# A two-layer graph network on one core: warm-up matmuls, a re-ordered start, GpSimd in the x split, and the last block in column halves

## The reference

```python
deg = jnp.sum(adj, axis=1, keepdims=True) + 1e-05            # layer 0
out = (adj / deg) @ h @ W_neigh.T + b_neigh + h @ W_self.T + b_self
x = layernorm(x + relu(out))
d = rowsum ** (-0.5)  (0 where rowsum is 0)                   # layer 1
x = layernorm(x + relu((d[:, None] * adj * d[None, :]) @ x @ W + b))
```

## Time and profile before

| what | us |
|---|---|
| median of 3 runs (lowest, highest) | 800.73 (800.4, 802.11) |
| span of the profiled execution, first to last instruction | 800.8 |
| busy: TensorE, VectorE, ScalarE, GpSimd | 782.1, 577.4, 386.9, 0.3 |
| the chain that ended last: TensorE's share | 94% |

### The profile page before, as it was taken

The page is one execution under the profiler, slowest core; times in us unless marked ns, Lnnn a source line. Parts: engine busy times, 40 slices in busy tenths (PEclk is TensorE's granted clock), DMA queues, the critical chain, the costliest instruction groups (busy, mean ns, idle before and its releaser), DMA issues.

```text
span 800.8 us, 11034 instructions
## 1 busy us (share of the span) xinstructions
PE 782.1 (98%) x3704; PEld 653.0 (82%) x3704; DVE 577.4 (72%) x868; ACT 386.9 (48%) x528; POOL 0.3 (0%) x6
## 2 busy tenths in 40 slices
PE   7899999999999999999999999999999999999995
PEld 4678888888888888888888888888888888888884
DVE  5799989899898998989966554555546455554643
ACT  3463745536446364454554545445444544545451
POOL 0000000000000000000000000000000000000000
PEclk9999999999999999999999999999999999999998
DMA  8767574755647556465565575746575574657540
GB/s 258 274 252 239 179 244 154 253 183 166 236 155 236 193 174 236 157 233 189 181 227 165 175 255 174 250 162 237 180 236 187 171 246 162 236 180 239 180 158 27
DMA packets 54459, 160.93 MB, mean 201 GB/s; under 512 B 5024, under 2 KB 18464, under 8 KB 54432
## 3 DMA queue, kind: packets, MB, share of 16 engines
q1 hardware_dynamic: 46224, 152.46, 56.6%
q10 hardware_dynamic: 8208, 8.13, 2.9%
HBM read 152.17 MB, written 8.39 MB: 201 GB/s over the span
## 4 chain that ended last, share of the span: by engine, by line
PE 94%; DMA 2%; DVE 2%; ACT 1%; issue 0%; SPq 0%
PE ps_main L675 84%; PE ps_epi L613 8%; DMA raw<-adj_t 2%; PE ps_main L657 1%; PE ps_epi L634 1%; DMA tt<-x_nat 1%; DVE lo L389 0%; DVE acc L565 0%; ACT hi L256 0%; PE ps_epi L693 0%; DVE tt L436 0%; DVE stats L585 0%; DVE tt L419 0%; DVE xs L389 0%; ACT tt L359 0%
## 5 line engine op out<-in xcount | busy, mean ns | idle before, releaser
L256 ACT ACTIVATE hi<-raw 128x1024 fp32r<-128x1024 f32 x254 | 269.4, 1061 | 352.8 <-PE ps_main L675 327.8
L389 DVE TENSOR_TENSOR lo<-raw,hi 128x1024 fp32r<-128x1024 f32 x254 | 310.4, 1222 | 145.3 <-ACT hi L256 145.2
L675 PE MATMUL ps_main<-hi,xs 128*128 128x512 f32 x1136 | 366.3, 392 | 4.3 <-DVE lo L389 4.3
L675 PE MATMUL ps_main<-hi,zs 128*128 128x512 f32 x896 | 283.0, 390 | 0.0
L675 PEld LDWEIGHTS ps_main<-hi,xs 128*128 128x128 f32 x1136 | 214.2, 189 | 49.3 <-DVE lo L389 3.6
L675 PE MATMUL ps_main<-lo,xs 128*128 128x512 f32 x568 | 222.4, 392 | 0.0
L675 PEld LDWEIGHTS ps_main<-hi,zs 128*128 128x128 f32 x896 | 168.3, 188 | 34.3
L675 PE MATMUL ps_main<-lo,zs 128*128 128x512 f32 x448 | 174.7, 390 | 0.0
L565 DVE TENSOR_TENSOR acc<-acc,raw 128x1024 f32<-128x1024 f32 x112 | 136.3, 1217 | 0.0
L675 PEld LDWEIGHTS ps_main<-lo,xs 128*128 128x128 f32 x568 | 107.3, 189 | 20.0 <-issue 0.2
L675 PEld LDWEIGHTS ps_main<-lo,zs 128*128 128x128 f32 x448 | 84.2, 188 | 16.3
(11 more groups left out here) (74 smaller groups left out, 322.7 us busy)
## 6 DMA issues: line engine op xcount, KB each, us to landing
raw<-adj_t SPq DMA_DIRECT2D x256, 512.0 KB, 3.3
res<-x_nat SPq DMA_DIRECT2D x11, 512.0 KB, 6.4
xt_sb<-xt SPq DMA_DIRECT2D x8, 512.0 KB, 5.0
x_scratch<-tt ACTq DMA_DIRECT2D x8, 512.0 KB, 6.2
res<-x_scratch SPq DMA_DIRECT2D x8, 512.0 KB, 6.0
out<-tt ACTq DMA_DIRECT2D x7, 512.0 KB, 6.4
tt<-x_nat SPq DMA_DIRECT2D x4, 512.0 KB, 6.4
acc<-x_nat SPq DMA_DIRECT2D x2, 256.0 KB, 3.6
```

The source lines that it names most:

```text
L256: return act.activation(dst, src, ACT.Copy)
L389: return dve.tensor_tensor(dst, src, hi_part.bitcast(f32), ALU.subtract)
L675: last = pe.matmul(ps[:, f, :], stationary(layer, part, jt, f), mov[:, slot(u), cols], start=(jt == 0 and i == 0), stop=(jt == JT - 1 and ...
```

## The change

- TensorE first runs seven matmuls of zeros (512 columns) into `ps_main[1]`, which is overwritten later. VectorE clears the tile they read.
- The first transfer of `adj` becomes two halves of 256 KB, issued first on SyncE; the three pieces of x's chunk 0 (128, 128 and 256 KB) are issued by ScalarE. TensorE's first units wait piece by piece.
- Weights are loaded behind unit 8's transfer instead of unit 4's and split at unit 8, the biases behind unit 12's; `xt` at unit 11 instead of 8, used at 11 instead of 10.
- The `lo` parts of chunks 3, 5, 7 and 0 are subtracted by GpSimd. Chunk 0 is split at the end of the first block, since only the second block reads its split form; VectorE and TensorE wait for it there.
- The last four units of the last block are multiplied in two column halves (256 columns each). The first half's product with `W` and its rows are done while the second half is being multiplied; the second half of units 0 to 11 is kept in `xt` by ScalarE and added by VectorE.

```diff
+HB = IB // 2
+HT = TB // 2
+TAIL = NU - RING
+WARM = 7
...
+        on_dve, on_pool = (1, 2, 4, 6), (3, 5, 7, 0)
+
+        def wait_x_split(eng, c):
+
+            if c in on_dve:
+                eng.wait_ge(xl_ready, on_dve.index(c) + 1)
+            else:
+                eng.wait_ge(xl_ready_pool, on_pool.index(c) + 1)
...
-            return 10 if is_first(b) else 9
+            return 11 if is_first(b) else 9
...
-                        load_x_first(0)
+                        sp.dma_start(raw[:, 0, 0:IB], adj_in[0, 0, :, 0:IB]).then_inc(raw_head, 16)
+                        sp.dma_start(raw[:, 0, IB:UW], adj_in[0, 0, :, IB:UW]).then_inc(raw_full[0], 16)
+                        continue
...
-                        if u == 0:
-                            load_x_first(1)
-                        elif u % 2 == 1 and u < NU - 1:
+                        if u % 2 == 1 and u < NU - 1:
                             load_x((u + 1) // 2)
-                        if u == 4:
+                        if u == 8:
                             load_weights()
+                        if u == 12:
+                            load_biases()
...
+            for c in on_pool:
+                at = slice(c * XC, (c + 1) * XC)
+                pool.wait_ge(xh_ready, c if c else JT // XC)
+                pool.tensor_tensor(xs[:, at, 1, :], x_stage(c), xs[:, at, 0, :].bitcast(f32), ALU.subtract)\
+                    .then_inc(xl_ready_pool, 1)
...
-                        if u % 2 == 0:
+                        if u % 2 == 0 and u > 0:
                             c = u // 2
-                            if c == 0:
-                                for full in x_first_full:
-                                    act.wait_ge(full, 16)
-                            else:
-                                act.wait_ge(x_full[c % 2], 16 * ((c + 1) // 2))
+                            act.wait_ge(x_full[c % 2], 16 * ((c + 1) // 2))
                             split_hi(xs[:, c * XC:(c + 1) * XC, 0, :], x_stage(c)).then_inc(xh_ready, 1)
-                        if u == 7:
+                        if u == NU - 1:
+                            for full in x_first_full:
+                                act.wait_ge(full, 16)
+                            split_hi(xs[:, 0:XC, 0, :], x_stage(0)).then_inc(xh_ready, 1)
+                        if u == 8:
...
+                def stationary_hi(f):
                     act.wait_ge(half_done, f + 1)
-                    split_hi(st_hi[:, f, :], ps_main[1][:, f, :]).then_inc(sth_ready, 1)
-                act.wait_ge(root_ready, 2 * NB)
-                act.activation(root[:, 0:TB], root_in[:, 0:TB], ACT.Sqrt).then_inc(root_taken, 1)
-                act.wait_ge(norm_ready, 2 * NB)
-                for t in range(TB // 2, TB):
+                    split_hi(st_hi[:, f, 0:HB], ps_main[1][:, f, 0:HB]).then_inc(sth_ready, 1)
+
+                def keep_partial(f):
+                    act.wait_ge(stl_ready, 2 * NB + f)
+                    act.activation(partial(f), ps_main[1][:, f, HB:IB], ACT.Copy).then_inc(part_ready, 1)
+
+                def stationary_hi_late(f):
...
+            for i, at in enumerate((slice(0, 1), slice(1, 2), slice(2, XC))):
+                act.dma_start(x_stage(0)[:, at, :], x_nat[0, :, at, :]).then_inc(x_first_full[i], 16)
...
+                stationary_lo(0)
+                stationary_lo(1)
+                rows(0)
+                add_partial(0)
+                stationary_lo_late(0)
+                scales(0)
+                add_partial(1)
+                stationary_lo_late(1)
+                rows(1)
+                scales(1)
+                dve.wait_ge(norm_ready, 2 * NB + 1)
+                dve.tensor_scalar(tt[:, HT, :], tt[:, HT, :], rstd[:, HT:HT + 1], nmr[:, HT:HT + 1],
+                                  ALU.mult, ALU.add).then_inc(y_ready, 1)
...
+            dve.memset(xs[:, JT - 1, :, :].bitcast(f32), 0.0).then_inc(warm_set, 1)
...
+                if epi is None:
+
+                    pe.wait_ge(warm_set, 1)
+                    for _ in range(WARM):
+                        pe.matmul(ps_main[1][:, 0, :], xs[:, JT - 1, 0, 0:P], xs[:, JT - 1, :, :].rearrange("p a f -> p (a f)"),
+                                  start=True, stop=True)
+                elif layer == 0:
+                    wait_x_split(pe, 0)
...
+                def half_unit(h, f, u):
+                    if (h, f) == (0, 0):
+                        pe.wait_ge(z_ready, UJ * (u + 1))
+                        pe.wait_ge(l_ready, g0 + (u + 1))
+                    for q in range(UJ):
+                        jt = u * UJ + q
+                        cols = slice(q * IB + h * HB, q * IB + (h + 1) * HB)
+                        for i, (part, mov) in enumerate(((0, hi), (0, lo), (1, hi))):
+                            last = pe.matmul(ps_main[1 - h][:, f, 0:HB], stationary(1, part, jt, f),
+                                             mov[:, slot(u), cols], start=(h == 1 and jt == TAIL * UJ and i == 0),
+                                             stop=(jt == JT - 1 and i == 2))
+                    if u == NU - 1:
+                        last.then_inc(half_done, 1)
+
+                def half_product(h, k):
+                    pe.wait_ge(stl_ready, n + 1 + h * FH + k)
+                    for t in range(h * HT, (h + 1) * HT):
+                        for q, (st, part) in enumerate(((st_hi, 0), (st_hi, 1), (st_lo, 0))):
                             last = pe.matmul(ps_epi[:, t, 0:F], st[:, k, t * P:(t + 1) * P],
                                              moving_weight(1, part, k),
                                              start=(k == 0 and q == 0), stop=(k == FH - 1 and q == 2))
                         if k == FH - 1:
                             last.then_inc(tile_done, 1)
+
+                for f in range(FH):
+                    for u in range(TAIL, NU):
+                        half_unit(0, f, u)
+                half_unit(1, 0, TAIL)
+                half_unit(1, 0, TAIL + 1)
+                half_product(0, 0)
+                half_product(0, 1)
+                half_unit(1, 0, TAIL + 2)
+                half_unit(1, 0, TAIL + 3)
+                for u in range(TAIL, NU):
+                    half_unit(1, 1, u)
+                half_product(1, 0)
+                half_product(1, 1)```

What stands where on the engines that wait or are waited for follows. First VectorE in the first block, before, from unit 6's `lo` to unit 8's (`xs` is a chunk of x, `wn_sb` and `ws_sb` are the weights, `acc` the row sums):

```order
L389 TENSOR_TENSOR lo<-raw,hi 128x1024
L565 TENSOR_TENSOR acc<-acc,raw 128x1024
L389 TENSOR_TENSOR wn_sb<-xt_sb,wn_sb 128x512
L389 TENSOR_TENSOR ws_sb<-xt_sb,ws_sb 128x512
L389 TENSOR_TENSOR lo<-raw,hi 128x1024
L565 TENSOR_TENSOR acc<-acc,raw 128x1024
L389 TENSOR_TENSOR xs<-res,xs 128x4x256
L389 TENSOR_TENSOR lo<-raw,hi 128x1024
```

More of the change, by code:

```diff
@@ L237, in last_epilogue @@
                 load_residual(*epi)
-                for t in range(TB // 2):
-                    sp.wait_ge(y_ready, t + 1)
+                for t in range(HT):
+                    sp.wait_ge(x1_ready, (2 * NB - 1) * TB + t + 1)
                     sp.dma_start(out[NB - 1, t], tt[:, t, :]).then_inc(tt_stored, 16)
+                sp.wait_ge(y_ready, 1)
+                sp.dma_start(out[NB - 1, HT], tt[:, HT, :]).then_inc(tt_stored, 16)
                 sp.wait_ge(tt_stored, (2 * NB + TB) * 16)
@@ new lines, in last_epilogue @@
+                stationary_hi(1)
+                keep_partial(0)
+                keep_partial(1)
+                square_root(0)
+                stationary_hi_late(0)
+                stationary_hi_late(1)
+                normalise(0, 0)
+                normalise(0, 1)
+                square_root(1)
+                normalise(1, TB - 1)
+                act.wait_ge(x1_ready, (2 * NB - 1) * TB + HT + 1)
+                act.dma_start(out[NB - 1, TB - 1], tt[:, TB - 1, :]).then_inc(tt_stored, 16)
@@ new lines, in stationary_lo_late, with statistics, rows @@
+                def stationary_lo_late(f):
+                    dve.wait_ge(sth_ready, n + 1 + FH + f)
+                    split_lo(st_lo[:, f, HB:IB], whole(f), st_hi[:, f, HB:IB]).then_inc(stl_ready, 1)
+                def statistics(t):
+                    linked(but=1 if t % HT == 0 else 0)
+                    link(dve.bn_stats(stats[:, t, :], tt[:, t, :]))
+                def rows(h):
+                    t = h * HT
+                    scale_product(layer, n, t)
+                    scale_product(layer, n, t + 1)
+                    add_residual(n, t)
+                    add_residual(n, t + 1)
+                    statistics(t)
+                    statistics(t + 1)
+                    linked()
+                    dve.bn_aggr(mv[:, t, :], stats[:, t, :])
+                    link(dve.bn_aggr(mv[:, t + 1, :], stats[:, t + 1, :]))
+                    linked()
+                    at = slice(t, t + HT)
```

(25 more changed lines are left out.)

96 lines of the change are left out of this document (51 added, 45 removed).

## The result

The change made the kernel slower: 807.78 us as the median of 10 runs, against 800.8 for the kernel before, also of 10. I had forecast 794.1. The runs fall in two groups: two of the ten took 800.6 and 800.7 us, the other eight 807.1 to 810.4. Each run's time is about 1.8 us above its own span (808.36 against 806.5 for the profiled one).

What follows compares the result with a forecast made beforehand. TensorE was taken as the bound, so only the start and the end could give anything. The terms -2.1 - 6.5 + 2.7 - 0.8 = -6.7 us, against 800.8, gave 794.1 us; range 790.9 to 799.0.

Steps and rivals of the forecast that it cites:

- GpSimd's four subtractions: First block: moving four `lo` subtractions from VectorE to GpSimd, priced at +2.3 us, +2.7 with VectorE's remaining work.
- h: Time VectorE stands still for one GpSimd subtraction; taken as 1.14 us, bounds 0 and 2.0.
- 3h - 1.1: First block: new TensorE waits if GpSimd is slow, plus 1.7 us for the falling clock.
- GpSimd stops VectorE for its whole time: Rival, first block: h = 2.0, a wait of 4.9 us at unit 8; chance 0.25.
- The full stop: Rival that GpSimd halts VectorE throughout each subtraction: 796.3 us, or 798.0 with the clock falling; chance 0.25.
- a free GpSimd: Rival, first block: GpSimd works beside VectorE freely, h under 0.5: 791.8 us; chance 0.28.
- VectorE's own part: First block to unit 8: VectorE's remaining operations make TensorE wait for `lo`, +0.4 us.
- The slower rival: GpSimd too slow for VectorE to feed TensorE, a loss from h = 2.9, 804.0 us at h = 4; slower 0.09.
- Weights and biases later, -6.5 us: First block: later loads remove three waits, about 4.8 us, and the slow clock behind unit 5's wait, 1.7 us.
- Warm-up and first operands, -2.1 us: Start: zeros raise the clock by 7.0 us and `adj` lands earlier; unit 2 at 12.55 instead of 14.67.
- the rival on the cold clock: Start: warm-up does nothing for the clock; 0 to 1.5 us seen, up to 795.5; inside the forecast's 0.36.
- The end in column halves, -0.8 us: Last four units of the last block to the end: 22.25 us plus 0.2 for semaphores, instead of 23.25.

Runs made afterwards that it cites:

- experiment 10: Changed kernel, but in the first block from unit 4 on VectorE waits for its own `lo` before adding the unit: 801.74 us, ratio 1.001.
- experiment 3: Changed kernel, but VectorE waits at units 5, 9 and 13 until GpSimd's subtraction is there: 801.32 us, ratio 1.0012.
- experiment 5: Changed kernel with GpSimd's four subtractions replaced by fills of the same places, nothing read: 795.38 us, ratio 0.9935.
- experiment 4: Kernel before the change with the last block's column halves alone: 801.02 us against 801.04, ratio 1.0013.
- experiment 9: Kernel before the change with only weights, biases and `xt` moved later: 796.75 us against 800.88, ratio 0.9947.
- experiment 1: Changed kernel with all eight x splits on VectorE and nothing on GpSimd: 796.38 us against 801.04, ratio 0.9952.
- experiment 2: Changed kernel with one small GpSimd subtraction (64 columns) ahead of all others: 807.97 us, ratio 1.0111.
- experiment 7: Kernel of experiment 1 (nothing on GpSimd) without the seven warm-up matmuls of zeros: 796.55 us, ratio 0.995.
- experiment 8: Kernel of experiment 1, weights' `lo` behind unit 8's, last block's first column half multiplied unit by unit: 795.77 us, ratio 0.9941.

## Why the prediction was wrong

**The step that failed** is the one on GpSimd's four subtractions: "how long one takes and for how much of that time, h, VectorE stands still", bounded by 0 and 2.0 us. Both prices were on VectorE's side. I gave GpSimd its turn whenever it asked. The runs show that it can get none for as long as VectorE goes from one two-operand operation to the next: 16.47 us for the first subtraction, of which 2.2 are its own. TensorE then waits on GpSimd, not on VectorE, and 3h - 1.1 has no term for that. The next sentence of the prediction even has that VectorE "is nearly without a gap here". That is the condition of the starvation, and I priced nothing for it.

**Once GpSimd is in**, "GpSimd stops VectorE for its whole time" is what happens: h = 2.2, a little above my upper bound of 2.0 from the fills. Rows of the changed kernel (3.43 instead of 1.22) and of experiment 10 (3.42) show it. The Trainium skill's exclusive lock (SBUF — State Buffer, the section on the two separate sides) agrees with both sides of this; so does the estimate of 2.25 us from its GPSIMD Engine Reference, section 3.1, with 2.26 measured. The Trainium skill's rule in that section of SBUF — State Buffer, that whoever starts first keeps the pair for its instruction, doesn't say who starts when VectorE's next operation is always ready. Here the rows show both: GpSimd shut out for thirteen operations (16.47 us), and GpSimd let in at the first boundary (52.85). The full stop was priced at 796.3 to 798.0 us, and it costs 801.3 and 801.7 (experiments 3 and 10). The wait up to unit 8 was nearly right: 1.54 us at unit 5 and 3.27 at unit 8 in experiment 10, 4.8 in all, where I had 4.9; and the granted clock stayed at 1.00 behind them, where it had been at 0.50 behind the 3.13 us of before. What I had left out is chunk 0's subtraction, which comes right behind chunk 7's and holds VectorE a fourth time (3.42 us for the addition at 56.64 in the changed kernel); TensorE waits 1.05 us for that pair in experiment 10 and 1.96 in experiment 3.

**The other terms** were too generous even without any hold: a free GpSimd was priced at 791.8 us, and with the fills of experiment 5, which hold nobody, it is 795.38. The paragraphs on the three terms below say where most of these 3.6 us are; besides, VectorE's own part was 1.6 us of waits there instead of the 0.4 that I had.

**The slower rival** named the right engine and the right sign, but its price was for a slow GpSimd, h of 2.9 or more. GpSimd isn't that slow, it is locked out. Its chance was 0.09, and that the sign came out its way says nothing for its mechanism.

**Weights and biases later, -6.5 us**: the mechanism is right to the row. No wait at unit 5, the transfer takes 3.67 us, the biases are hidden. Alone it brings 4.1 us by the medians (800.88 to 796.75). Spans agree with the larger number (800.8 to 794.6), because the profiled execution of before was one of the slower ones: with the 1.8 us that every run adds, its span of 800.8 stands for about 802.6 (an estimate, since its time is not on record), not for the median of 800.8. I had set the span equal to the median, 0.07 us apart. Experiment 4 has the kernel before's first block in a faster execution (span 799.1): TensorE waits 3.2 us for `lo` there instead of 4.3, and the split of the first block's result starts at 61.53 instead of 63.18. In experiment 9 it starts at 57.01, so by that pair the term is 4.5 us, not 6.5.

**Warm-up and first operands, -2.1 us**: unit 2 started at 13.15 in the changed kernel and 12.68 in experiment 1, against 12.55 predicted, so the size is nearly right in these two. When the clock comes up is no fixed time: I took 7.0 us, worked out from the kernel before. After the same zeros from 1.47 the pace of 0.43 us begins at about 5 in experiment 1, at 7.69 in the changed kernel and at 10.52 in experiment 2, where unit 2 starts at 14.41. Without zeros it begins at 8.7 in experiment 7 and at 11.2 before. And the term doesn't add to the others. Without GpSimd, VectorE is the slower engine up to unit 8, and experiment 7 shows 0.2 us by the medians for the whole warm-up, nothing that can be told. I had used this very argument for the rival on the cold clock and not for the sum.

**The end in column halves, -0.8 us**: 0.2 by the profiles, nothing by the times. I left out that feature half by feature half means passing all four units within 2.9 us, so the last unit's `lo` is wanted while VectorE is still at it (a wait of 0.41 us). With units in the outer loop (experiment 8) the end takes 22.4 us and the predicted 0.8 is there.

**What stays open** is what decides whether GpSimd gets in at once. In the profiles ten subtractions or copies asked while a VectorE operation ran and got in right behind it: seven with no gap recorded there, two (experiment 10) with one of 0.03 us and one (experiment 2) with one of 0.88. Six others did not, and none of these got in later before VectorE stood still, up to thirteen operations on. Nothing in the rows tells the two kinds apart. With it stays open why 2 of the changed kernel's 10 runs took 800.6 us. A chance gap in VectorE's list, as in experiment 2's chunk 3, or a first boundary that lets GpSimd in would do it, and it is near the time of experiments 3 and 10. No profile of such a run was taken, so this is argued, not shown.

## What to carry to other kernels

Before giving GpSimd a share of VectorE's work, look at VectorE's timeline at that place: where it goes without a gap from one operation with two SBUF operands to the next, a GpSimd operation that reads SBUF can be kept out until VectorE stands still, and whoever waits for its result waits with it. Where it gets its turn, the GpSimd operation still stops VectorE for its whole length, so it pays only when that is shorter than what VectorE is spared. Small transfers that nobody needs yet are worth moving away from the start; that was nearly the whole gain here. And terms that are won on one engine are not to be added before it is clear which engine bounds the stretch once they are won.

## What the runs showed of the hardware that I had not expected

- A 128x1024 float32 subtraction on GpSimd takes 2.2 to 2.3 us once it has its turn (2.26 in experiment 3), a copy 1.04, a fill 0.96; the same subtraction on VectorE 1.22.
- Beside a gapless list of two-operand VectorE operations a subtraction took 16.47 us and a copy 15.38, while four fills took 0.96 each. Others got in at the first boundary of such a list: chunk 7's in the changed kernel, chunk 5's in experiment 2. A GpSimd operation either got in there or waited until VectorE stood still.
- With VectorE's additions starting 1.25 instead of 1.14 us behind their `lo`, no subtraction took over 3.5 us and no run of eleven was slow (experiment 10).
- After the same seven matmuls of zeros TensorE's faster pace began anywhere from about 5 us (experiment 1) to 10.52 us (experiment 2). The granted clock fell to 0.50 behind a wait of 3.13 us in the kernel before, and stayed at 1.00 behind one of 3.27 us in experiment 10.
